# One new order for five engines, and no cleared spare words behind 71 indirect transfers, in an attention and expert kernel

## The chip, the cores and the metric

The kernel runs on one core of a Trainium2 chip. The metric is the device time of one launch in microseconds (us). Before the change it is 222.59 us, the median of three runs (222.12 to 223.31).

The engines are TensorE (PE, matrix products), VectorE (DVE), ScalarE (ACT), GpSimd (POOL) and SyncE (SP, which here only issues DMA). Each runs its own list of instructions in order, and semaphores tie the lists together.

## The reference

The input is normalised row by row. Causal attention over two batches of 2048 rows of 128, and a routed feed-forward layer of 8 experts, both read the normalised rows, and both are added to the input.

```python
def _L0_attn_ref(input_data, qk, ov):
    scores = jnp.einsum('bsd,de,bte->bst', input_data, qk, input_data) / SCALE
    scores = jnp.where(causal, scores, -jnp.inf)
    attn = jax.nn.softmax(scores, axis=-1)
    return jnp.einsum('bst,btd,de->bse', attn, input_data, ov)
...
def _L0_ffn_ref(input_features, centroids, ln_g, ln_b, w1, b1, w2, b2):
    x = input_features.reshape(-1, D)
    eid = jnp.argmax(x @ centroids.T, axis=-1)
    alpha = jax.nn.sigmoid(jnp.sum(x * centroids[eid], axis=-1, keepdims=True))
    xln = normalised(x) * ln_g[eid] + ln_b[eid]
    h = jax.nn.relu(xln @ w1[e] + b1[e])          # for the row's own expert e
    ffn = h @ w2[e] + b2[e]
    return x + alpha * ffn
...
x = L0_attn_input_data
xn = _layernorm(x, axis=-1)
x = x + _L0_attn_ref(xn, L0_attn_qk, L0_attn_ov) + _L0_ffn_ref(xn, ...)
```

The first listing lines are condensed: the layer applies only the expert that a row has chosen.

## The kernel before

The 4096 rows are 32 tiles of 128, in 8 groups of 4 tiles (4 groups for each batch).

**Attention.** A step n (0 to 79) takes one tile of keys against one group of 512 queries. In the order it is X.n (PE, scores in three 16-bit products), EH.n and EX.n (ACT, the exponential in 16 and in 32 bits), XL.n (DVE, the remainder `p_lo`, line 910), P.n and PB.n (PE, weights times values, lines 1343/1344 and 1351). A group of queries first needs its row maxima: M.b.g.i.c is one PE product, MR of the same indices its maximum by DVE (lines 892 and 896), RM.b.g gathers them, and SH/SHa write the shift into the queries. QT.b.g.f divides one half of a group by its sums and frees its banks. Keys, queries and values come by T, Q and V on PE, Ta, Qa, Va on ACT, Tl, Ql, Vl on DVE.

**Routing.** AFF and AFFr (PE), CH (DVE, choice of experts), CNT (PE), PL (DVE, each row's place in the sorted buffer). Then `send_rows` (SC.0 to SC.31 on POOL) scatters each tile of rows to `sorted_x` in HBM by an indirect DMA (line 684).

**Experts.** Once all 32 scatters have landed, SP issues transposing loads (`x2T`, line 526). For 39 tiles of sorted rows, HI.k is the first product (lines 1434 to 1436), RE.k and LO.k make its two 16-bit halves (ACT line 1166, DVE line 1018), OUT.k is the second product (lines 1456 to 1462), YS.j scales two tiles (ACT line 1174), and `store_rows` (SO.0 to SO.38 on POOL) scatters a tile to `sorted_y` (line 693). When all 39 have landed, SP loads the results back (line 568), Y.g adds a group (DVE line 937), and SP stores it.

**What sets the order.** ORDER is one list of 1120 entries, written out by hand or by a planner. Each engine walks the whole list and carries out the entries that are its own, so the list fixes the order within each engine and nothing between engines: semaphores do that. SP walks it too, for loads and clears that hang on W1, W2l and Z.

**The lines that the change touches.** `transfer_before` makes a scatter wait until the third scatter before it has landed (APART is 3). `pass_time` clears 600 words of `v_full`, in one partition, on POOL behind each of the 71 scatters; the next scatter stands behind that in POOL's list. `v_full` is no longer read by then: the first clear waits for that.

Other names of the prediction: VAR.g0.g1 are the statistics of groups g0 to g1 (DVE lines 778 and 781), LE their logarithm and root on ACT, RN the last step of the root (DVE for groups 0 to 1, POOL otherwise, lines 710 to 718), ROW the normalised rows by DVE (line 799), BIASa and BIAS the split of the biases (ACT lines 1095/1096, DVE lines 960/962), BASE a sum on POOL (line 641), MISC constants on POOL. W2l.e is the remainder of the second matrix of expert e on POOL (line 735): it reads two tensors in SBUF. W2.e is the ACT step ahead of it, and the matrices share three buffers, so SP loads the one of expert e+3 when W2l.e is done.

Of the kernel before, what the change touches and what calls it, by code (L numbers as in the profile page):

```python
# [1495 lines left out]
```

## Time and profile before

| | us |
|---|---|
| median of three runs | 222.59 |
| the profiled execution | 222.64 |
| its span, first to last instruction | 220.9 |
| PE busy | 205.3 (93%) |
| DVE busy | 176.3 (80%) |
| ACT busy | 155.2 (70%) |
| POOL busy | 155.0 (70%), of which the 71 clears 41.8 |

All later numbers are on the scale of the span, which starts at the first instruction. 1.7 us of the time lie around it. A busy PE includes the tail of each pipelined product, so a product of 512 columns is listed with 0.38 us although the next starts 0.22 us after it. To know the work of PE, take the distance from start to start.

### The profile page before, as it was taken

The page shows a single profiled execution, that of the slowest core. Times are in us where ns is not written, and L with a number is a line of the kernel's source. Part 1 is how long each engine was busy: PE and PEld are TensorE (multiplying, and loading weights), DVE is VectorE, ACT ScalarE, POOL GpSimd, SP SyncE. Part 2 cuts the span into 40 slices and gives each one's busy share as a digit, 9 for nine tenths or more (in the row PEclk, how much of TensorE's full clock was granted, in tenths as well). Part 3 has the DMA queues.
Part 4 walks back from the last instruction along what each step waited for, and adds up shares of the span by engine and source line. Part 5 has one row for each costly group of instructions (what it writes and reads, how often), then busy time and mean ns, then how long its engine had stood idle before and what let it go on. Part 6 is the DMA issues. An engine that isn't in the chain of part 4 may idle for free.

```text
span 220.9 us, 6878 instructions
## 1 busy us (share of the span) xinstructions
PE 205.3 (93%) x2428; PEld 159.0 (72%) x2428; DVE 176.3 (80%) x448; ACT 155.2 (70%) x346; POOL 155.0 (70%) x230
## 2 busy tenths in 40 slices
PE   7798875999979999999999989999999999999993
...
DVE  6799999898999999999999864576547674635995
...
GB/s 171 291 291 92 3 0 95 189 374 149 3 24 38 37 39 39 39 36 41 36 43 34 127 184 159 113 154 117 122 178 75 39 39 50 29 40 154 283 206 131
DMA packets 37601, 23.55 MB, mean 107 GB/s; under 512 B 12472, under 2 KB 34144, under 8 KB 37568
## 3 DMA queue, kind: packets, MB, share of 16 engines
...
q10 hardware_dynamic: 336, 0.14, 0.3%
...
## 4 chain that ended last, share of the span: by engine, by line
PE 77%; DVE 12%; ACT 4%; issue 4%; DMA 1%; SPq 1%; DVEq 0%; ACTq 0%
PE psum L1343 6%; PE psum L1300 6%; PE psum L1302 6%; PE psum L1301 6%; PE psum L1351 6%; PE psum L1344 6%; PE psum L1277 5%; PE psum L1462 4%; PE psum L1461 4%; PE psum L1460 4%; PE psum L1434 4%; PE psum L1436 4%; PE psum L1435 4%; PE psum L1260 3%; PE psum L1334 2%
## 5 line engine op out<-in xcount | busy, mean ns | idle before, releaser
L910 DVE TENSOR_TENSOR p_lo<-p_sb,p_hi 128x512 f16<-128x512 f32 (+1 forms) x68 | 42.0, 640 | 12.0 <-ACT p_sb L1050 11.8
L1044 ACT ACTIVATE p_hi<-psum 128x512 f16<-128x512 f32 (+1 forms) x68 | 37.1, 547 | 19.4 <-PE psum L1351 14.2
L1050 ACT ACTIVATE p_sb<-psum 128x512 f32<-128x512 f32 (+1 forms) x80 | 42.5, 538 | 6.8 <-PE psum L1334 6.7
L693 POOL DMA_INDIRECT sorted_y<-xn x39 | 38.6, 989 | 10.9 <-issue 5.4
L1018 DVE SCALAR_TENSOR_TENSOR h_lo<-psum,h_hi 128x512 f16<-128x512 f32 x39 | 26.8, 691 | 21.0 <-ACT h_hi L1166 19.4
L684 POOL DMA_INDIRECT sorted_x<-xr,pos x32 | 33.5, 1047 | 11.9 <-issue 11.4
L671 POOL MEMSET v_full<- 1x600 f32 x71 | 41.8, 589 | 0.0
L1166 ACT ACTIVATE h_hi<-psum 128x512 f16<-128x512 f32 x39 | 23.3, 597 | 19.6 <-PE psum L1436 17.3
L1343 PE MATMUL psum<-v_hi,p_hi 128*128 128x129 f16 x236 | 32.7, 220 | 1.2 <-DVE x_sb L927 1.2
L896 DVE TENSOR_REDUCE row_max<-psum 128x1 f32<-128x512 f32 x48 | 32.3, 684 | 1.6 <-PE psum L1277 1.1
L1344 PE MATMUL psum<-v_lo,p_hi 128*128 128x128 f16 x236 | 32.6, 219 | 0.0
L1277 PE MATMUL psum<-kT_hi,qT_hi 128*128 128x512 f16 (+3 forms) x80 | 26.3, 349 | 4.2 <-DVE row_max L896 1.8
L1434 PE MATMUL psum<-x2T,w_hl 128*128 128x128 f16 x156 | 28.0, 219 | 0.2 <-issue 0.2
L1462 PE MATMUL psum<-w_hl,h_lo 128*128 x156 | 28.1, 219 | 0.0
L1461 PE MATMUL psum<-w_hl,h_hi 128*128 x156 | 28.1, 219 | 0.0
L1460 PE MATMUL psum<-w_hl,h_hi 128*128 x156 | 28.1, 219 | 0.0
L1436 PE MATMUL psum<-x2T,w_hl 128*128 128x128 f16 x156 | 28.0, 219 | 0.0
L1435 PE MATMUL psum<-x2T,w_hl 128*128 128x128 f16 x156 | 28.0, 219 | 0.0
L1300 PE MATMUL psum<-qT_hi,kT_hi 128*128 128x512 f16 (+1 forms) x80 | 27.8, 347 | 0.0
L1302 PE MATMUL psum<-qT_hi,kT_lo 128*128 128x512 f16 (+1 forms) x80 | 27.8, 347 | 0.0
L1301 PE MATMUL psum<-qT_lo,kT_hi 128*128 128x512 f16 (+1 forms) x80 | 27.8, 347 | 0.0
L1343 PEld LDWEIGHTS psum<-v_hi,p_hi 128*128 128x128 f16 x236 | 23.0, 98 | 4.1 <-DVE x_sb L927 1.3
(189 smaller groups left out, 527.4 us busy)
## 6 DMA issues: line engine op xcount, KB each, us to landing
...
sorted_y<-xn POOLq DMA_INDIRECT x39
sorted_x<-xr,pos POOLq DMA_INDIRECT x32
```

What stands on the lines that cost most here:

```text
L671: pool.memset(idle, 0.0).then_inc(s_idle, 1)
L693: pool.indirect_dma_start(out=sorted_y[:, :], out_offset=bass.IndirectOffsetOnAxis(ap=tokens, axis=0), in_=xs[:, t % SLOTS, 0:P], in_offse ...
L910: v.tensor_tensor(p_lo[:, u, off:GW], p_sb[:, u, off:GW], p_hi[:, u, off:GW], ALU.subtract).then_inc(s_plo, 1)
L1044: a.activation(p_hi[:, u, off:GW], bank[SCORE[n % R]][:, off:GW], ACT.Exp, scale=SCALE).then_inc(s_exph, 1)
L1050: a.activation(p_sb[:, u, off:GW], bank[SCORE[n % R]][:, off:GW], ACT.Exp, scale=SCALE).then_inc(s_exp, 1)
L1277: mm(at[:, 0:w], qT_hi[:, q:q + P], kT_hi[:, k:k + w], start=True, stop=True).then_inc(s_mm, 1)
L1300: mm(at[:, off:GW], kT_hi[:, kk], qT_hi[:, q], start=True, stop=False)
L1301: mm(at[:, off:GW], kT_hi[:, kk], qT_lo[:, q], start=False, stop=False)
L1302: m = mm(at[:, off:GW], kT_lo[:, kk], qT_hi[:, q], start=False, stop=not diag)
L1343: mm(to[i], w, v_hi[:, kt, 0:P + 1], start=(j == 0 and i % 2 == 0), stop=False, skip_group_check=True)
L1344: mm(to[i][:, 0:P], w, v_lo[:, kt, :], start=False, stop=False, skip_group_check=True)
L1460: mm(to, h_hi[:, h, at], hi, start=False, stop=False, skip_group_check=True)
```

## The change

`pass_time`, its semaphore `s_idle`, the view `idle` and the constant IDLE go, and with them the 71 POOL memsets and the waits around them. ORDER has the same 1120 entries as before in another order, for all engines. No entry is added or dropped, and no function but the two scatter helpers changes.

```diff
 ORDER = entries("""
-VAR.0.1 VAR.1.2 BIASa LE.0.1 C0a AE.0 WU C0 C1 C2 T.0 W1.0 W1.1 BIAS RN.0.1 ROW.0.1 RN.1.2 MISC BASE.0 BASE.1 RN.2.3
-Vl.0 RN.3.4 BASE.2 RN.4.6 T.1 AE.1 AE.2 C1a LE.1.2 C2a Ta.0 W1h.0 W1h.1 Ta.1 W1l.0 Qa.0 Vf.0 LE.2.3 AE.3 W1l.1 AE.4
...
-M.0.3.0.3 P.6 AFFr.1.3 SH.0.2 M.0.3.3.2 X.11 V.2 P.7 CNT P.8 X.12 P.9 X.13 P.10 MR.0.3.3.2 Vl.2 QT.0.1.0 QT.0.1.1
-MR.0.3.1.3 XL.12 XL.13 MR.0.3.0.1 MR.0.3.2.2 Sl.1 MR.0.3.2.3 MR.0.3.3.3 MR.0.3.0.2 XL.14 MR.0.3.1.2 MR.0.3.3.0 X.14
-P.11 M.0.3.0.1 M.0.3.1.3 P.12 X.15 M.0.3.2.2 P.13 PB.12 M.0.3.3.3 M.0.3.2.3 X.16 M.0.3.0.2 PB.13 X.17 M.0.3.1.2 P.14
...
-SC.27 SC.28 SC.29 SC.30 SC.31 W2l.5 W2l.6 W2l.7 Sl.5 MR.1.1.3.0 XL.27 XL.28 XL.29 MR.1.1.1.1 MR.1.1.0.0 MR.1.1.3.1
...
-LO.1 M.1.3.3.0 X.51 PB.47 P.49 PB.48 P.50 PB.49 P.51 HI.0 PB.50 PB.51 HI.1 HI.2 OUT.0 LO.2 MR.1.3.1.0 MR.1.3.1.3 LO.3
...
-X.66 P.64 X.67 PB.63 XL.54 XL.55 XL.56 XL.57 XL.58 XL.59 XL.60 XL.61 XL.62 XL.63 XL.64 XL.65 XL.66 XL.67 Y.6 XL.68 Y.0
...
-SO.31 SO.32 SO.33 SO.34 SO.35 SO.36 SO.37 PB.70 X.73 P.72 PB.71 X.74 P.73 X.75 PB.72 X.76 PB.73 X.77 P.74 PB.74 X.78
-X.79 P.75 PB.75 P.76 PB.76 P.77 EH.77 EX.77 EH.78 EX.78 PB.77 P.78 P.79 PB.78 EH.79 EX.79 QT.1.3.0 QT.1.3.1 SO.38 PB.79
+VAR.0.1 VAR.1.2 LE.0.1 LE.1.2 C0a C1a BIASa C2a AE.0 Ta.0 Ta.1 AE.1 AE.2 AE.3 AE.4 W1h.0 LE.2.3 LE.3.4 W1h.1 AE.5 WU C0
+C1 C2 T.0 T.1 W1.0 W1.1 RN.0.1 ROW.0.1 C1v ROW.1.2 C2v BIAS Tl.0 VAR.2.3 VAR.3.4 Tl.1 MISC RN.1.2 RN.2.3 RN.3.4 BASE.0
...
+X.11 X.12 X.13 P.10 P.11 V.2 M.0.3.2.3 X.14 X.15 X.16 P.12 P.13 PB.12 PB.13 X.17 P.14 PB.14 P.15 M.0.3.0.0 M.0.3.0.1
...
+P.19 M.0.3.1.2 M.0.3.2.1 X.21 X.22 V.3 V.4 Q.4 PB.18 X.23 P.20 PB.19 PB.20 P.21 Vl.1 S.7 SC.0 SC.1 SC.2 W2l.2 W2l.3 SC.3
+SC.25 SC.26 SC.27 SC.28 SC.29 SC.30 SC.31 W2l.4 W2l.5 W2l.6 W2l.7 MR.1.0.1.0 Sl.4 RM.1.0 MR.1.1.0.1 MR.1.1.1.1 MR.1.1.3.1
...
+PB.44 PB.45 X.48 X.49 P.46 P.47 M.1.2.2.2 PB.46 X.50 X.51 P.48 PB.47 PB.48 REG M.1.2.1.2 P.49 P.50 P.51 HI.0 PB.49 PB.50
+PB.51 HI.1 HI.2 OUT.0 OUT.1 M.1.2.2.1 HI.3 HI.4 M.1.2.1.1 OUT.2 HI.5 OUT.3 HI.6 M.1.2.2.0 OUT.4 OUT.5 M.1.3.0.0 HI.7
...
+XL.59 XL.60 XL.61 XL.62 Y.6 Y.0 XL.63 XL.64 XL.65 XL.66 Y.7 Y.3 XL.67 XL.68 QT.1.2.0 XL.69 XL.70 QT.1.2.1 XL.71 XL.72
...
+PB.71 P.72 P.73 PB.72 X.75 X.76 PB.73 X.77 P.74 P.75 PB.74 X.78 PB.75 P.76 PB.76 X.79 P.77 PB.77 P.78 P.79 PB.78 EH.76
+EX.75 EX.76 EH.77 EH.78 EX.77 EX.78 EH.79 EX.79 QT.1.3.0 QT.1.3.1 SO.38 PB.79
 """)
...
-    IDLE = 600
...
-        idle = flat(v_full[:])[0:1, 0:IDLE]
...
-        s_idle = sem("s_idle")
...
-            pauses = [0]
-
-            def pass_time():
-
-                if pauses[0]:
-                    pool.wait_ge(s_idle, pauses[0])
-                else:
-                    pool.wait_ge(s_pv, N_FULL)
-                    pool.wait_ge(s_vhi, FULL)
-                    pool.wait_ge(s_vlop, FULL)
-                pool.memset(idle, 0.0).then_inc(s_idle, 1)
-                pauses[0] += 1
-
             def send_rows(i):
...
                 transfers.append((s_sent[i % SENT], 16 * (i // SENT + 1)))
-                pass_time()
 
             def store_rows(t):
...
                 transfers.append((s_yst[t % DUMPS], 16 * (t // DUMPS + 1)))
-                pass_time()
```

## Rows read from the trace of the kernel before

**Rows 1.** Page, part 2: busy tenths in 40 slices of 5.5 us.

```profile
PE   7798875999979999999999989999999999999993
DVE  6799999898999999999999864576547674635995
```

**Rows 2.** Windows by stage: length, then busy us (instructions) of each engine.

```profile
core 0: us, PE busy (x) PEld busy (x) DVE busy (x) ACT busy (x) POOL busy (x), PEclk, DMA share, GB/s
4.00:58.00 54.00, 46.38 (x342) 28.89 (x340) 49.99 (x176) 40.39 (x100) 35.05 (x70) 0.97 0.52 159
...
63.60:124.50 60.90, 60.38 (x659) 43.64 (x660) 58.34 (x134) 46.61 (x99) 52.79 (x65) 1.00 0.15 43
124.50:128.10 3.60, 2.31 (x39) 2.14 (x40) 3.16 (x9) 2.51 (x5) 1.16 (x1) 1.00 1.13 99
128.10:181.70 53.60, 53.59 (x930) 52.35 (x931) 32.45 (x55) 31.57 (x71) 45.87 (x59) 1.00 0.52 121
181.70:216.00 34.30, 34.30 (x405) 25.78 (x403) 22.76 (x42) 27.34 (x60) 15.55 (x20) 1.00 0.46 128
```

**Rows 3.** Timeline of PE, around P.12 and OUT.0: start us, duration us, line.

```profile
63.59 0.23 PE L1343 MATMUL psum<-v_hi,p_hi 128*128 128x129 f16 x1 [1.16 <-DVE x_sb L927]
...
64.06 0.38 PE L1300 MATMUL psum<-qT_hi,kT_hi 128*128 128x512 f16 x1
64.27 0.38 PE L1301 MATMUL psum<-qT_lo,kT_hi 128*128 128x512 f16 x1
...
128.10 0.10 PEld L1456 LDWEIGHTS psum<-b_hl,pick 128*128 x1 [1.46 <-issue]
```

**Rows 4.** Page, part 5: the cleared spare words.

```profile
L671 POOL MEMSET v_full<- 1x600 f32 x71 | 41.8, 589 | 0.0
```

**Rows 5.** Timeline of POOL: two scatters one after the other.

```profile
67.81 0.97 POOL L684 DMA_INDIRECT sorted_x<-xr,pos  x1 [0.17 <-issue]
...
69.53 0.97 POOL L684 DMA_INDIRECT sorted_x<-xr,pos  x1 [0.17 <-issue]
```

**Rows 6.** Line 684, POOL idle before it until an earlier scatter landed (us, times).

```profile
  DMA sorted_x<-xr,pos: 0.3, 2
```

**Rows 7.** Timeline of DVE, the first 20 us.

```profile
6.93 0.68 DVE L960 SCALAR_TENSOR_TENSOR b_hl<-b_sb,b_hi 16x512 f16<-16x512 f32 x1 [0.59 <-ACT b_hi L1096]
...
7.74 0.14 DVE L768 SCALAR_TENSOR_TENSOR nt<-mv,r 128x4 f32<-128x4 f32 x1
...
8.31 1.11 DVE L799 TENSOR_SCALAR xn<-x_sb,mv,r 128x127 f32<-128x127 f32 x4
...
11.21 3.01 DVE L799 TENSOR_SCALAR xn<-x_sb,mv,r 128x127 f32<-128x127 f32 x4
...
19.91 0.26 DVE L892 CUSTOM_DVE_ANT_0 masked<-psum,late_keys 128x128 f16<-128x128 f32 x1
```

**Rows 8.** Timeline of ACT, the wait for the biases.

```profile
5.88 0.72 ACT L1095 ACTIVATE b_hi<-b_sb,lower_half 16x512 f16<-16x512 f32 x1 [3.81 <-DMA b_sb<-in_L_ffn_b]
```

**Rows 9.** Timeline of POOL, its idle time before RN.1.2, and BASE.0.

```profile
9.34 0.24 POOL L710 TENSOR_SCALAR nt<-mv 128x4 f32<-128x4 f32 x1 [4.84 <-ACT r L1061]
...
12.41 1.16 POOL L641 TENSOR_TENSOR x_sb<-x_sb,xn 128x508 f32<-128x508 f32 x1
```

**Rows 10.** Timeline of DVE: start of PL, XL.47 to XL.49, LO.0 to LO.2.

```profile
58.02 0.16 DVE L849 TENSOR_SCALAR tiles_f<-psum 128x8 f32<-128x8 f32 x1
...
120.11 3.25 DVE L910 TENSOR_TENSOR p_lo<-p_sb,p_hi 128x512 f16<-128x512 f32 x3
...
126.24 1.93 DVE L1018 SCALAR_TENSOR_TENSOR h_lo<-psum,h_hi 128x512 f16<-128x512 f32 x3
```

**Rows 11.** Timeline of POOL: W2l.5 and W2l.6.

```profile
119.38 2.26 POOL L735 TENSOR_TENSOR w_hl<-w_raw,w_hl 128x512 f16<-128x512 f32 x2
```

**Rows 12.** Line 910 by itself, 62 to 80 us: duration ns minimum, median, maximum.

```profile
L910 DVE TENSOR_TENSOR p_lo<-p_sb,p_hi x8: 682/684/687, 63.8 to 78.5; 128x512 f16<-128x512 f32 x8
```

**Rows 13.** Timeline of SP: the eight loads of the results.

```profile
199.59 5.73 SPq L568 DMA_DIRECT2D xn<-sorted_y  x8
```

**Rows 14.** Timeline of ACT: EH.78, third exponential from the end.

```profile
215.73 0.38 ACT L1044 ACTIVATE p_hi<-psum 128x256 f16<-128x256 f32 x1 [0.41 <-PE psum L1351]
```

More of the change, by code:

```diff
@@ L129 @@
-X.79 P.75 PB.75 P.76 PB.76 P.77 EH.77 EX.77 EH.78 EX.78 PB.77 P.78 P.79 PB.78 EH.79 EX.79 QT.1.3.0 QT.1.3.1 SO.38 PB.79
+VAR.0.1 VAR.1.2 LE.0.1 LE.1.2 C0a C1a BIASa C2a AE.0 Ta.0 Ta.1 AE.1 AE.2 AE.3 AE.4 W1h.0 LE.2.3 LE.3.4 W1h.1 AE.5 WU C0
+C1 C2 T.0 T.1 W1.0 W1.1 RN.0.1 ROW.0.1 C1v ROW.1.2 C2v BIAS Tl.0 VAR.2.3 VAR.3.4 Tl.1 MISC RN.1.2 RN.2.3 RN.3.4 BASE.0
+BASE.1 BASE.2 RN.4.6 Vf.0 Qa.0 Qa.1 Z.0 RN.6.8 BASE.3 BASE.4 BASE.5 Vl.0 BASE.6 BASE.7 COL0 S.0 S.1 S.2 W2l.0 S.3 S.4
+S.5 S.6 W2l.1 VAR.4.6 Ql.0 Ql.1 MR.0.0.0.0 V.0 Q.0 Q.1 Z.1 Z.2 MR.0.0.2.0 MR.0.0.3.0 MR.0.0.1.0 VAR.6.8 RM.0.0 Z.3
@@ new lines @@
+M.0.0.0.0 W1b.0 W1b.1 M.0.0.2.0 M.0.0.3.0 M.0.0.1.0 W1.2 V.1 T.2 W1.3 M.0.1.0.1 W1b.2 M.0.1.1.1 M.0.1.2.0 Tl.2
+MR.0.1.0.1 MR.0.1.1.1 ROW.4.6 MR.0.1.3.1 MR.0.1.2.0 ROW.6.8 MR.0.1.1.0 MR.0.1.3.0 W1l.4 W1l.5 MR.0.1.2.1 Ql.2 MR.0.1.0.0
+R2 RM.0.1 MR.0.2.0.2 MR.0.2.2.1 MR.0.2.0.1 MR.0.2.3.1 MR.0.2.3.2 MR.0.2.2.0 W1l.0 W1l.1 XA.2 LE.4.6 W1h.2 Vf.1 Ta.2
+W1h.3 LE.6.8 W1l.2 W1l.3 Va.0 SHa.0.0 XA.3 W1h.4 W1h.5 Qa.2 EX.0 EX.1 EX.2 XA.5 SHa.0.1 XA.7 R2a EX.3 EX.4 W2.0 Ta.3
+Ta.4 EX.5 EX.6 Ta.5 Ta.6 Qa.3 Ta.7 W1b.3 M.0.1.3.1 SH.0.0 W1.4 W1.5 M.0.1.1.0 M.0.1.3.0 X.0 Q.2 M.0.1.2.1 X.1 X.2
@@ new lines @@
+M.0.3.1.2 M.0.3.2.1 X.21 X.22 V.3 V.4 Q.4 PB.18 X.23 P.20 PB.19 PB.20 P.21 Vl.1 S.7 SC.0 SC.1 SC.2 W2l.2 W2l.3 SC.3 SC.4
+SC.5 SC.6 SC.7 SC.8 SC.9 SC.10 SC.11 SC.12 SC.13 SC.14 SC.15 SC.16 SC.17 SC.18 SC.19 SC.20 SC.21 SC.22 SC.23 SC.24 SC.25
+SC.26 SC.27 SC.28 SC.29 SC.30 SC.31 W2l.4 W2l.5 W2l.6 W2l.7 MR.1.0.1.0 Sl.4 RM.1.0 MR.1.1.0.1 MR.1.1.1.1 MR.1.1.3.1
+XL.29 XL.30 XL.31 Sl.5 MR.1.1.1.0 Sl.6 XL.32 MR.1.1.2.1 MR.1.1.3.0 XL.33 MR.1.1.0.0 XL.34 XL.35 MR.1.1.2.0 RM.1.1 XL.36
+MR.1.2.0.0 MR.1.2.3.1 XL.37 XL.38 XL.39 MR.1.2.3.0 QT.0.3.0 QT.0.3.1 Sl.7 XL.40 XL.41 SH.0.3 P.22 P.23 V.5 V.6 V.7 PB.21
@@ new lines @@
+PB.44 PB.45 X.48 X.49 P.46 P.47 M.1.2.2.2 PB.46 X.50 X.51 P.48 PB.47 PB.48 REG M.1.2.1.2 P.49 P.50 P.51 HI.0 PB.49 PB.50
+PB.51 HI.1 HI.2 OUT.0 OUT.1 M.1.2.2.1 HI.3 HI.4 M.1.2.1.1 OUT.2 HI.5 OUT.3 HI.6 M.1.2.2.0 OUT.4 OUT.5 M.1.3.0.0 HI.7
+HI.8 OUT.6 HI.9 OUT.7 M.1.3.3.3 HI.10 OUT.8 HI.11 OUT.9 OUT.10 HI.12 HI.13 OUT.11 HI.14 OUT.12 HI.15 OUT.13 M.1.3.2.2
+HI.16 M.1.3.2.3 OUT.14 HI.17 OUT.15 HI.18 OUT.16 HI.19 OUT.17 HI.20 OUT.18 OUT.19 M.1.3.0.3 HI.21 M.1.3.1.3 OUT.20
+SH.1.2 HI.22 HI.23 OUT.21 HI.24 OUT.22 OUT.23 M.1.3.0.1 HI.25 HI.26 OUT.24 HI.27 OUT.25 EX.46 W1h.7 Qa.7 W2.5 EH.47
```

89 lines of the change are left out of this document (38 added, 51 removed).

## The prediction

> **What bounds the kernel now.** First the tenths of busy time [rows 1]: PE is near full from slice 13 (about 66 us) to slice 39, with one dent at slice 23. Ahead of that it isn't, but DVE is, from slice 3 on. Then the windows [rows 2]: from 4 to 58 us DVE is busy 49.99 of 54.00 and PE 46.38, and much of that is listed tails. From 63.6 to 124.5 both are full (60.38 and 58.34 of 60.90). From 128.1 to 216 PE has no gap and DVE has a third free. Then what ends PE's idle time [rows 3]: P.12 waits 1.16 us for DVE (QT.0.1.1 frees the banks of the sums), and OUT.0 starts at 128.10 after 1.46 us for the first LO and the loading of expert numbers.
>
> So I count PE's work. A product of 512 columns takes 0.216 us from start to start (64.06 to 64.27 [rows 3]), one of 128 columns a quarter of that. The same products are made before and after, so the end moves by two things alone: by how much work PE has done at a given time in the first 128 us, and by the tail. I use three marks: the start of PL on DVE (58.02 [rows 10]), P.12 (63.59) and OUT.0 (128.10 [rows 3]).
>
> **The change, part by part.**
>
> *The clears.* 71 memsets of 0.589 us, 41.8 us in all, leave POOL [rows 4]. A scatter follows the one before at 1.72 us: 0.97 for itself, 0.59 for the memset, 0.17 of waiting [rows 5]. Without the memset I take 0.97 + 0.17 = 1.14. The wait for the third scatter before bound twice in 32, for 0.3 us in all [rows 6], at a distance of three times 1.72. At 1.14 it may bind more, so the bounds of the spacing are 1.14 and 1.72. I take 1.2. That gives 38 us for 32 scatters instead of 55. From PL they would run to about 102, and HI.0 needs them at about 120: some 18 us of cover. Even at 1.72 they would end near 120. Worth by itself: 0. In the expert phase a tile takes PE 1.4 us (53.6 us [rows 2] for nearly 39 tiles), so the second set of scatters would follow PE and end near 187, and SP's loads would start near 189 instead of 199.59 [rows 13]. DVE wants them (Y.6 after XL.62) near 194, where before it stood after XL.67. Cover about 1 us, worth 0.
>
> Does DVE gain when the memsets go? XL takes 682/684/687 ns between memsets [rows 12]: no spread, no gain. The Trainium skill (SBUF — State Buffer, Who interferes with whom) says why: a DVE instruction with two SBUF inputs contends with a GpSimd instruction that reads SBUF, not with one that only writes. By that rule the clears are harmless, and W2l, which reads, isn't.
>
> *The head.* Now DVE waits 0.59 us for ACT's split of the biases [rows 7], which itself waits 3.81 us for its DMA [rows 8], and RN.0.1 starts behind BIAS at 7.74 [rows 7]. In the new order LE.0.1 and BIAS change places: RN.0.1 can start when VAR.1.2 is done, at about 6.3. That is 1.4 us sooner, of which 0.6 is a wait that vanishes and the rest is BIAS work moved behind. ROW.1.2 takes 3.01 us for four tiles where ROW.0.1 takes 1.11 [rows 7], and POOL's BASE.0 runs beside it [rows 9]. In the new order ROW.1.2 comes at about 9 us, when POOL waits between two RN (it sits idle for 4.84 us ahead of 9.34 now [rows 9], and MISC goes there). I take 1.11 for it: 1.9 less. Together 2.5. Walking DVE's list from there with a spacing of 0.6 us for each 512-column operation, I reach MR.0.0.0.0 at 18.1 with one more operation (Ql.1) done ahead of it, against 19.91 [rows 7]: 2.4 gained. Going on to PL, which has the same amount of DVE work ahead in both orders, I meet two new waits: CH.0 for the affinities (0.4) and the tighter ACT list around W2.3. I keep 1.6: PL at 56.4. Bounds: 0 (the chain over ACT takes it back) and 2.4.
>
> *More PE work ahead of P.12.* The new order puts X.15 and X.16 ahead of P.12: six products of 512 columns, 1.30 us, and 0.1 of maxima. This fills the 1.16 us wait [rows 3]. P.12 itself moves with QT.0.1.1 to about 62.0. So at P.12 PE's idle time so far would be 1.6 + 1.4 = 3.0 us less.
>
> *P.12 to OUT.0.* Seven M units and their MR go behind HI.0, with Ql.7 and RM.1.2 on DVE (1.4 us of PE, 3.2 of DVE ahead of LO.0). Against that, DVE starts this stretch with less done (X.15, X.16 and their XL are ahead on PE only). Adding up the entries, DVE needs 57.7 us from QT.0.1.1 to LO.0 where it needed 60.2, and PE 58.7 from P.12 to OUT.0 where it needed 61.5. Before, DVE lost 2.5 us in this stretch. I keep that loss: LO.0 at 62.0 + 57.7 + 2.5 = 122.2, and OUT.0 1.9 later as before (126.24 to 128.10 [rows 10, 3]): 124.1. PE's work ahead of OUT.0 is 1.4 less, so the net gain is 128.1 - 124.1 - 1.4 = 2.6 us.
>
> *W2l beside XL.* Before, three W2l stood behind the scatters. W2l.5 and W2l.6 ran from 119.38 to 121.64 [rows 11], and three XL took 3.25 us there [rows 10], where three spacings of 0.6 and a tail make 1.9: 1.4 lost. Now W2l.2 and W2l.3 stand after SC.2 and W2l.4 after SC.31, so three more run while XL runs. Bounds: 0 (DVE is at an operation that reads PSUM) and 3 x 1.4 = 4.2. I take 0.6, since DVE's loss counts only where PE waits for it and two of five of its operations there are XL.
>
> *After OUT.0.* PE has no gap in 88 us [rows 2], and the seven M units stand among 39 tiles, with DVE free for a third. Cost 0; if LO came late behind an MR it would be up to 0.6 at a time. *The tail.* X.79 stands behind P.75 to PB.76, 1.35 us of products later, and EH.78 ahead of EX.77. EH.78 already waits 0.41 for PE [rows 14]; then EX.77, EX.78, EH.79, EX.79, XL.79 and PB.79 must follow. I make it 0.3 longer; bounds 0 and 0.8.
>
> **Sum:** -2.6 + 0.6 + 0.3 = -1.7 us. The profiled execution took 222.64, so 220.9; the median of the runs (222.59) is the same to 0.1. Forecast 220.9.
>
> **The rivals.**
>
> *The head's gain is taken back (no change).* For it: ACT's list up to EX.8 is full too, and each step of my walk took the earliest time. Then PL starts at 58.0, P.12 near 63.5, and only the fuller PE list remains, 1.4 less 0.9 for tail and W2l: 222.1.
>
> *W2l against XL (slower).* Three XL beside two W2l lost 1.4 us [rows 10, 11]. (The Trainium skill, SBUF — State Buffer, Who interferes with whom, has this as a rule: whichever starts first holds the port, the other fully blocks. This trace agrees, with that one case.) If all three added W2l hit an XL while PE and DVE are both full, and those behind SC.31 hit as before, the cost is 4.2 instead of 0.6: 220.9 + 3.6 = 224.5. It decides from a loss of about 3.5 us on DVE between P.12 and LO.0 on top of the 2.5 it has. Against it: DVE's operations in between read PSUM, and only a start within the 1.13 us of a W2l counts. The list in pairs (two EH, then two EX) could lose time at the same place, by XL starting an ACT operation (0.5 us) later; the buffers are three, so I find no step where PE must wait for it, but it adds to this case.
>
> *The scatters don't come closer.* If the wait for the third before binds at each, the spacing stays near 1.7. The first set still has cover of about 0, the second ends near 192, Y.6 would wait 4 us, and PE with it for some 3 once its three buffers are full: 223.9.
>
> *The whole head gain holds and nothing is lost:* 2.4 instead of 1.6, and no W2l loss: 219.5.
>
> **How the numbers follow.** Forecast with its own spread (219.5 to 221.5, the last rival within): 0.55. Gain taken back (221.5 to 223): 0.22. W2l, or pairs, slower: 0.15, near 224.5. Scatters not closer: 0.08, near 223.9. The likeliest gives 220.9. The range reaches below to a head and a middle both better than walked (218.3) and above to the two slower cases in part (224.0), leaving out 0.2. A measurement of this kernel can tell about 0.5%, 1.1 us: faster means below 221.5, slower above 223.7. From the cases: faster 0.58, same 0.25, slower 0.17.
>
> **What would show each step.** ROW.1.2 at about 9 us in 1.1 us; PL near 56.4; P.12 near 62.0 without a wait; scatters 1.14 to 1.2 us apart, the first set ending near 102 and SP's loads of results near 189; OUT.0 near 124; no XL over 1.3 us. The prediction is wrong if PL starts at 58 or later, if PE waits between P.12 and HI.0 by more than 2 us, if an XL of 2 us appears more than once, or if Y.6 waits for its load.

## The result, and the profile after

The changed kernel takes 215.03 us (median of 4 runs, 214.78 to 216.25) where the kernel before took 222.57 beside it: ratio 0.967, 95% interval 0.963 to 0.971. The forecast of 220.9 had the direction right and was 5.9 us too slow, and 215.03 lies outside its range (218.3 to 224.0). The profiled execution is the slowest of the four, 216.25, with a span of 214.5. Executions more than 1.5% above the fastest of their kernel are left out of all medians and ratios below (one of b1, one of b3, four of c6).

Lines of the changed kernel stand 2 to 3 lower up to 655 and 16 to 18 lower behind (L910 is now L892, L799 is L781). First the page of the changed kernel, part 2, in 40 slices of 5.4 us (before: [rows 1]):

```profile
PE   7979999999999999999998799999999999999993
...
DVE  6899899999999999999998586646577574667784
...
PEclk9996999999999999999999999999999999999999
```

Slices are counted from 0. DVE is full from slice 2, and PE's dent comes in slices 21 and 22 instead of 23. PEclk (granted clock in tenths of 2.4 GHz) has a dip at slice 3. Then the windows by stage, as in [rows 2]:

```profile
core 0: us, PE busy (x) PEld busy (x) DVE busy (x) ACT busy (x) POOL busy (x), PEclk, DMA share, GB/s
4.00:52.60 48.60, 45.20 (x337) 29.12 (x335) 46.06 (x172) 36.78 (x92) 29.53 (x64) 0.96 0.46 141
52.60:57.90 5.30, 5.20 (x41) 3.18 (x39) 4.92 (x19) 5.02 (x13) 2.24 (x2) 1.00 0.54 175
57.90:116.10 58.20, 56.99 (x643) 42.18 (x644) 56.06 (x129) 48.30 (x103) 39.37 (x36) 1.00 0.20 60
116.10:120.00 3.90, 2.50 (x46) 2.33 (x44) 3.22 (x11) 3.01 (x6) 2.32 (x2) 1.00 0.94 190
120.00:173.30 53.30, 53.26 (x909) 51.32 (x910) 32.99 (x57) 29.73 (x69) 30.54 (x32) 1.00 0.50 115
```

The stretch up to PL is 5.4 us shorter, the one up to OUT.0 much as before. The marks are rows of the timelines of DVE (start of RN.0.1, ROW.0.1, ROW.1.2, ROW.6.8, PL) and PE (P.12, OUT.0), which answer to [rows 7], [rows 10] and [rows 3]; columns are start, duration, line and, in brackets, the idle time before:

```profile
6.00 0.16 DVE L750 SCALAR_TENSOR_TENSOR nt<-mv,r 128x4 f32<-128x4 f32 x1
6.59 1.11 DVE L781 TENSOR_SCALAR xn<-x_sb,mv,r 128x127 f32<-128x127 f32 x4
8.38 1.10 DVE L781 TENSOR_SCALAR xn<-x_sb,mv,r 128x127 f32<-128x127 f32 x4
25.78 1.11 DVE L781 TENSOR_SCALAR xn<-x_sb,mv,r 128x127 f32<-128x127 f32 x4
52.61 0.15 DVE L831 TENSOR_SCALAR tiles_f<-psum 128x8 f32<-128x8 f32 x1
```

```profile
57.92 0.23 PE L1325 MATMUL psum<-v_hi,p_hi 128*128 128x129 f16 x1
119.98 0.23 PE L1438 MATMUL psum<-b_hl,pick 128*128 128x128 f16 x1 [1.40 <-DVE h_lo L1000]
```

| mark, us from the start of the span | before | predicted | after |
|---|---|---|---|
| PL starts | 58.02 | 56.4 | 52.6 |
| P.12 | 63.59 | 62.0 | 57.92 |
| OUT.0 | 128.10 | 124.1 | 119.98 |
| OUT.0 to the end of the span | 92.8 | 94.5 | 94.5 |
| scatters, first set, last one starts | 117.8 | about 101 | 108.5 |
| SP's loads of results | 199.59 | 189 | 184.41 |

Behind P.12 the forecast of the marks holds almost to the tenth. Of the 5.9 us of the miss, 3.8 stand ahead of PL and 0.3 between PL and P.12; the other 1.8 are a term beside the marks (0.6) and the distance from the profiled execution to the median (1.2).

The scatters of the first set, by what GpSimd waited for before each, and the timeline of DVE and POOL where the pair W2l.4, W2l.5 meets XL (as in [rows 10, 11]):

```profile
L668 POOL DMA_INDIRECT sorted_x<-xr,pos x32: 954/958/1909, 62.5 to 108.5; - x32
...
  issue: 9.3, 13
  DMA sorted_x<-xr,pos: 5.9, 18
```

```profile
108.46 5.02 DVE L892 TENSOR_TENSOR p_lo<-p_sb,p_hi 128x512 f16<-128x512 f32 x4
```

```profile
109.44 2.28 POOL L717 TENSOR_TENSOR w_hl<-w_raw,w_hl 128x512 f16<-128x512 f32 x2
```

Four XL take 5.02 us where four alone take about 2.5. One of them, started at 109.11, takes 3166 ns by itself: the prediction wanted none over 1.3 us.

### The profile page after: what moved, and what is told of

The parts are those of the page before. It is cut to its first block, busy times and chain, and to the rows that moved or that the text cites. A ratio compares the mean times of both kernels' runs of the same rounds, so it can differ in the third digit from the quotient of the medians.

```text
span 214.5 us, 6806 instructions
## 1 busy us (share of the span) xinstructions
PE 203.2 (95%) x2428; PEld 158.5 (74%) x2428; DVE 173.0 (81%) x448; ACT 154.4 (72%) x346; POOL 113.7 (53%) x159
## 4 chain that ended last, share of the span: by engine, by line
PE 76%; DVE 17%; issue 5%; ACT 1%; DVEq 0%; ACTq 0%
PE psum L1333 6%; PE psum L1325 6%; PE psum L1259 6%; PE psum L1326 5%; PE psum L1284 5%; PE psum L1283 5%; PE psum L1282 5%; PE psum L1442 4%; PE psum L1444 4%; PE psum L1443 4%; PE psum L1418 4%; PE psum L1416 4%; PE psum L1417 4%; DVE row_max L878 3%; PE psum L1242 3%
## 5 line engine op out<-in xcount | busy, mean ns | idle before, releaser
L676 POOL DMA_INDIRECT sorted_y<-xn x39 | 37.4, 958 | 26.9 <-ACT xn L1156 14.7
L892 DVE TENSOR_TENSOR p_lo<-p_sb,p_hi 128x512 f16<-128x512 f32 (+1 forms) x68 | 41.9, 653 | 11.3 <-ACT p_sb L1032 11.0
L1026 ACT ACTIVATE p_hi<-psum 128x512 f16<-128x512 f32 (+1 forms) x68 | 35.7, 540 | 13.6 <-PE psum L1333 11.2
L668 POOL DMA_INDIRECT sorted_x<-xr,pos x32 | 34.8, 1088 | 15.5 <-issue 9.3
L1032 ACT ACTIVATE p_sb<-psum 128x512 f32<-128x512 f32 (+1 forms) x80 | 38.8, 537 | 3.0 <-PE psum L1286 3.0
L878 DVE TENSOR_REDUCE row_max<-psum 128x1 f32<-128x512 f32 x48 | 31.6, 681 | 1.0 <-PE psum L1259 0.7
L1325 PE MATMUL psum<-v_hi,p_hi 128*128 128x129 f16 x236 | 31.3, 220 | 0.1
L1326 PE MATMUL psum<-v_lo,p_hi 128*128 128x128 f16 x236 | 31.2, 219 | 0.0
L1259 PE MATMUL psum<-kT_hi,qT_hi 128*128 128x512 f16 (+3 forms) x80 | 25.0, 353 | 3.2 <-issue 1.0
L1416 PE MATMUL psum<-x2T,w_hl 128*128 128x128 f16 x156 | 27.6, 219 | 0.0
L1417 PE MATMUL psum<-x2T,w_hl 128*128 128x128 f16 x156 | 27.6, 219 | 0.0
L1418 PE MATMUL psum<-x2T,w_hl 128*128 128x128 f16 x156 | 27.6, 219 | 0.0
L1326 PEld LDWEIGHTS psum<-v_lo,p_hi 128*128 128x128 f16 x236 | 23.1, 98 | 1.6
```

What stands on the lines that cost most here:

```text
L676: pool.indirect_dma_start(out=sorted_y[:, :], out_offset=bass.IndirectOffsetOnAxis(ap=tokens, axis=0), in_=xs[:, t % SLOTS, 0:P], in_offse ...
L878: v.tensor_reduce(row_max[:, i, c:c + 1], bank[bank_of[unit]][:, 0:w], AX.X, ALU.max).then_inc(s_max, 1)
L892: v.tensor_tensor(p_lo[:, u, off:GW], p_sb[:, u, off:GW], p_hi[:, u, off:GW], ALU.subtract).then_inc(s_plo, 1)
L1032: a.activation(p_sb[:, u, off:GW], bank[SCORE[n % R]][:, off:GW], ACT.Exp, scale=SCALE).then_inc(s_exp, 1)
L1259: mm(at[:, 0:w], qT_hi[:, q:q + P], kT_hi[:, k:k + w], start=True, stop=True).then_inc(s_mm, 1)
L1325: mm(to[i], w, v_hi[:, kt, 0:P + 1], start=(j == 0 and i % 2 == 0), stop=False, skip_group_check=True)
```

## Experiments: the clears and the order, each without the other

**Only the clears go.**

```diff
 ORDER = entries("""
-(the new order)
+(the order of before, all 1120 entries)
 """)
```

> The changed kernel with the order of before: only the clears are gone. Theory (the clears are worth nothing by themselves; before, the last scatter of the first set starts at 117.8 and HI.0 at 124.5, with slack over the load): the scatters come 1.2 to 1.3 us apart and the first set ends near 106, but DVE's marks stay: Tl.0 and PL within 0.3 us of before (PL 58.0), HI.0 near 124.5, time 222.3 (221.5 to 223.0). Rival (the clears on GpSimd slow DVE or hold the start of the experts): 215 to 218.5, with OUT.0 4 us or more earlier than 128.1.

Measured 225.63 us, ratio 1.013 (1.011 to 1.015): 3 us slower than before. Neither theory had that. PL starts at 57.2, but there is a new loss at 110 to 118 us, in the timelines of POOL, DVE and PE of this run:

```profile
110.48 2.27 POOL L717 TENSOR_TENSOR w_hl<-w_raw,w_hl 128x512 f16<-128x512 f32 x2
```

```profile
110.08 3.44 DVE L892 TENSOR_TENSOR p_lo<-p_sb,p_hi 128x384 f16<-128x384 f32 x2
```

```profile
113.24 0.34 PE L1333 MATMUL psum<-v_hi,p_lo 128*128 128x129 f16 x3 [1.41 <-DVE p_lo L892]
...
114.17 1.32 PE L1242 MATMUL psum<-w_raw,A_e 128*128 128x512 f32 x2 [0.36 <-DVE w_hl L964]
115.29 0.63 PE L1244 MATMUL psum<-b_hl,pick_first 128*128 128x512 f16 x1
```

and its windows around that:

```profile
111.40:115.30 3.90, 2.12 (x18) 1.05 (x16) 3.87 (x7) 1.53 (x4) 1.35 (x2) 0.96 0.31 72
115.30:118.50 3.20, 3.20 (x13) 1.53 (x12) 1.80 (x7) 0.62 (x2) 0.00 (x0) 0.52 0.93 115
```

Without the clears the scatters end at 110.5, so W2l.5 and W2l.6 run from 110.48 instead of 119.38 [rows 11]. One XL is held through both (its own duration is 3103 ns), PE waits 1.41 us for it, is busy for only 2.12 of 3.90 us, and then gets 0.52 of its clock (that is, nearly all at 1.2 GHz) for 3.2 us: 512 columns take 0.63 us instead of 0.38.

**The clears are back, but where they delay only that pair.**

```diff
                 transfers.append((s_sent[i % SENT], 16 * (i // SENT + 1)))
-                pass_time()
+                if i == NT - 1:
+                    for _ in range(16):
+                        pass_time()
 ...
                 transfers.append((s_yst[t % DUMPS], 16 * (t // DUMPS + 1)))
-                pass_time()
```

> The old order with no clears between the scatters, but with 16 clears in a row (9.4 us) behind the last scatter of the first set, so that W2l.5 and W2l.6 come near 120 as they did before, and not near 110.5. With the old order and no clears at all they ran at 110.48, one XL took about 2.8 us, PE waited 1.41 for it and fell to 1.2 GHz for some 2.5 us: 225.6 against 222.6. Theory (that collision alone is the loss of 3 us): no XL over 1.9 us near 110, no fall of PE's clock there, time 221.5 to 222.6. Rival (scatters closer together are slower for the rest in another way): 224.5 or more.

Measured 222.86 us, ratio 1.000 (0.997 to 1.003), 0.26 above the top of the theory's interval and clearly not the rival. The windows of the same two stretches:

```profile
111.40:115.30 3.90, 3.90 (x39) 2.57 (x37) 3.86 (x10) 2.30 (x6) 3.64 (x6) 1.00 0.14 43
115.30:118.50 3.20, 3.20 (x29) 1.99 (x28) 2.93 (x10) 2.21 (x5) 2.91 (x6) 1.00 0.72 104
```

PE is busy throughout and keeps 2.4 GHz. So the 3 us are the collision and the clock after it, and the clears are worth nothing by themselves with the old order: taking them away only brings W2l to a worse place. The Trainium skill (SBUF — State Buffer, Who interferes with whom) says of GpSimd and a DVE operation with two SBUF inputs that the two can contend; the 3103 ns agree. Who started first did not decide it here: this XL started at 110.08, 0.40 us ahead of W2l.5 at 110.48, and it was XL that waited, while the two W2l took 1.17 and 1.15 us as ever. The same shows in all eight runs with an XL over 3 us (XL first by 0.33 to 0.41 us, though starts on POOL are rough), so the prediction's rule that the one that starts first blocks the other isn't borne out by them.

**Only the order changes.**

```diff
-                transfers.append(...)
+                transfers.append(...)
+                pass_time()
```

> The kernel of before with the new order: the clears stay. Theory (the order gives the gain up to PL, and the clears would then hold the start of the experts): PL stays near 52.6, but the scatters come 1.72 us apart from 62.5 and W2l.2 and W2l.3 stand among them, so the last starts near 118 instead of 108.5; the loads of the first expert tile follow and HI.0 starts near 123.5 instead of 116.1, so the time is 221 to 224, that is, the gain of the order shows only without the clears. Rival A (the order alone is the cause and the scatters have slack): 215 to 216.5, with HI.0 below 118. Rival B (DVE's marks up to 52.6 us need the clears gone): PL at 56 or later.

Measured 236.25 us, ratio 1.061 (1.058 to 1.065). PL starts at 51.1 and the last scatter at 119.9, as expected, but the loss of 21 us was nearly three times the expected one. The two halves of it were then taken apart.

```diff
 # in the first of the two runs send_rows alone has this line, in the second store_rows alone
+                pass_time()
```

> The new order with the clears kept in the first set of scatters only (32 of 71). With all 71 the kernel took 236.25 us: HI.0 waited 11.2 us for its load, started at 126.9 with TensorE at 1.2 GHz until about 131.8, and near the end PE waited 6.3 us behind Y.6. Theory (the two sets cost separately; the first set's clears cost the wait at HI.0 and the clock after it): last scatter near 120, HI.0 near 127, OUT.0 near 131.8, no wait at Y.6 beyond that, time 226 to 229. Rival (the first set has cover and the loss is the second set's): 215 to 217.5.

> The mirror: clears only in the second set (39 of 71). Theory: OUT.0 stays at 120, the second set takes 1.7 us for each scatter from 123.9, so its last starts near 190 instead of 182.0, the loads of results and Y.6 follow near 198 instead of 190.9, XL queues behind Y.6 and PE waits some 5 us with a drop of its clock: 221 to 224. Rival (the second set has cover): 215 to 217.

Clears in the first set alone: 228.13 us, ratio 1.024 (1.022 to 1.027), in the theory's interval. PE's wait ahead of HI.0 and the windows around it:

```profile
126.66 0.29 PE L1433 MATMUL psum<-x2T,w_hl 128*128 128x128 f16 x1 [11.04 <-DMA x2T<-sorted_x]
```

```profile
115.00:126.70 11.70, 0.66 (x13) 0.49 (x10) 0.89 (x5) 1.74 (x4) 9.24 (x11) 0.60 0.26 70
126.70:131.60 4.90, 4.57 (x42) 4.36 (x42) 2.95 (x9) 1.71 (x4) 1.15 (x1) 0.55 1.02 175
```

HI.0 comes 6.8 us behind the start of the last scatter (119.9). That isn't the scatter's own time alone: in the new order SP has a load of raw weights ahead of HI.0's load, and that load is issued just behind the end of W2l.4 (122.53), which stands right behind SC.31. Both in the timeline of SP of this run:

```profile
122.56 0.37 SPq L503 DMA_DIRECT2D w_raw<-in_L_ffn_w  x1
123.10 1.30 SPq L526 DMA_TRANSPOSE x2T<-sorted_x  x1
```

So HI.0's load is issued 3.2 us behind the start of the last scatter here, 2.7 in the changed kernel and 2.4 in the kernel before. It takes about 3 us to land: at 114.3 in the changed kernel, 1.8 ahead of HI.0 (116.1), and at 123.0 in the kernel before, 1.4 ahead of HI.0 (124.5). Before, too, there was this little cover: with a PE list that is ready for HI.0 some 8 us sooner, the clears use it up.

Clears in the second set alone: 224.98 us (ratio 1.008, 1.004 to 1.013; runs from 222.7 to 225.9), above the theory's interval of 221 to 224 in the median. Its profiled execution has a span of 222.9. The waits of DVE (Y.6, Y.7) and PE there:

```profile
195.61 0.69 DVE L936 TENSOR_TENSOR x_sb<-x_sb,xn 128x512 f32<-128x512 f32 x1 [6.06 <-DMA xn<-sorted_y]
198.51 0.69 DVE L936 TENSOR_TENSOR x_sb<-x_sb,xn 128x512 f32<-128x512 f32 x1 [2.21 <-DMA xn<-sorted_y]
```

```profile
199.46 0.29 PE L1350 MATMUL psum<-v_hi,p_lo 128*128 128x129 f16 x1 [7.83 <-DVE p_lo L909]
```

XL queues behind Y.6 on DVE, PE behind XL, and from 196 to 202 PE's granted clock is 0.54. The two halves together (13.1 and 10.0 over 215.03) make the 21.2 us of all 71 to within 2.

So the two parts of the change are worth -7.6 together, +3 (the clears alone) and +13.6 (the order alone).

## Experiments: what makes PL earlier

**Old head in the new order, and new head in the old order.**

```diff
 # a3: first entries of each engine as before
-VAR.0.1 VAR.1.2 LE.0.1 LE.1.2 C0a C1a BIASa C2a AE.0 Ta.0 Ta.1 AE.1 AE.2 ...
+VAR.0.1 VAR.1.2 BIASa LE.0.1 C0a AE.0 WU C0 C1 C2 T.0 W1.0 W1.1 BIAS RN.0.1 ROW.0.1 RN.1.2 MISC BASE.0 BASE.1 T.1 AE.1
+AE.2 C1a LE.1.2 C2a Ta.0 W1h.0 W1h.1 Ta.1 C2v C1v Tl.0 ROW.1.2 ...
 # a4: the reverse, all behind Tl.0, AE.2, RN.1.2 and W1.1 as before
```

> The changed kernel with the entries of the first 12 us (DVE to ROW.1.2, ACT to Ta.1, GpSimd to BASE.1, PE to T.1) back in the old order. After against before, DVE's time at an entry less the work listed ahead of it is 1.9 us better at Tl.0, 3.1 at R2 and 5.3 at PL. Theory (both halves count: the head gives about 2.5 us, the lists from 13 to 52 us give the rest by themselves): ROW.1.2 is at 11.2 and takes about 3 us again, PL near 55.0, time near 217.5 (216.5 to 218.5). Rival A (all is the head, and the later lists only pass it on): PL near 58, time 220.5 or more. Rival B (all is the later lists, and the head's gain would be caught up anyway): PL within 0.5 of 52.6, time below 216.

> The mirror: no clears, the order of before, but with the entries of the first 12 us (DVE to Tl.0, ACT to AE.2, GpSimd to RN.1.2, PE to W1.1) in the new order. Theory (both halves count): ROW.1.2 near 8.4 in 1.1 us, PL near 55.5 instead of 58.0, time near 220.0 (219.0 to 221.0). Rival A (all is the head): PL near 53, time 217 or less. Rival B (the head's gain is caught up again in the old lists): PL 57.5 or later, time 222 or more.

Old head: 218.23 us, ratio 0.984 (0.978 to 0.991), within the theory's interval, and the timeline of DVE shows ROW.1.2 held again and PL 1.9 us later than after:

```profile
11.38 3.01 DVE L781 TENSOR_SCALAR xn<-x_sb,mv,r 128x127 f32<-128x127 f32 x4
```

```profile
54.53 0.15 DVE L831 TENSOR_SCALAR tiles_f<-psum 128x8 f32<-128x8 f32 x1
```

The time is 3.2 us up, not 1.9. The profiled execution of the changed kernel had PE at 0.76 of its clock from 14 to 20 us and a3's at 0.97; where the new head and lists ran without it, PL is at 51.1 to 51.7, about 3 us ahead of this 54.5.

New head in the old lists: 224.14 us, where the old order without clears has 225.63. PL starts at 57.5, so nothing of the head is left there (57.2 without it). At ROW.4.6 the new head is still 1.45 us ahead of the old order without clears (28.21 against 29.66), although BASE.0 held BIAS for 1 us (1677 ns instead of 670): the gain goes between 30 and 57 us. DVE waits 1.2 us for PE's scores, 0.6 for kT_hi and 0.5 for the affinities on the way, together 1.1 more than in the old order without clears. Rival B was right for this run, the theory for the other: the head's gain lasts only with the new lists behind it.

**One cause put back: GpSimd's BASE beside ROW.1.2.**

```diff
-ROW.0.1 C1v ROW.1.2 C2v BIAS Tl.0 VAR.2.3 VAR.3.4 Tl.1 MISC RN.1.2 RN.2.3 RN.3.4 BASE.0 BASE.1
+ROW.0.1 C1v MISC RN.1.2 BASE.0 BASE.1 ROW.1.2 C2v BIAS Tl.0 VAR.2.3 VAR.3.4 Tl.1 RN.2.3 RN.3.4
```

> The changed kernel with one thing put back: GpSimd's BASE.0 and BASE.1 (1.16 us each, two SBUF inputs, back to back) stand beside DVE's ROW.1.2 again, here at about 8.4 us. Theory (the 3.01 us of ROW.1.2 before is one of its four operations held through both BASE, and that delay goes on to the end): ROW.1.2 takes 2 to 3 us again instead of 1.10, PL starts 1 to 1.9 us later than 52.6 and the kernel takes 216.0 to 217.0. Rival (ROW.1.2 was slow for another reason, or the delay is caught up at the next wait): ROW.1.2 1.1 us, or slow but PL within 0.3 of 52.6 and the time 215.0 (within 0.5).

Measured 217.53 us, ratio 0.977 (0.970 to 0.984), 0.5 above the theory's interval. The timelines of DVE and POOL, from the slowest execution (221.06):

```profile
8.31 1.94 DVE L781 TENSOR_SCALAR xn<-x_sb,mv,r 128x127 f32<-128x127 f32 x4
...
10.44 1.61 DVE L942 SCALAR_TENSOR_TENSOR b_hl<-b_sb,b_hi 16x512 f16<-16x512 f32 x1
```

```profile
8.23 1.18 POOL L638 TENSOR_TENSOR x_sb<-x_sb,xn 128x508 f32<-128x508 f32 x1
10.33 1.17 POOL L638 TENSOR_TENSOR x_sb<-x_sb,xn 128x508 f32<-128x508 f32 x1 [0.93 <-DVE xn L781]
```

BASE.1 waits for ROW.1.2 here, so the two BASE are apart and each holds one DVE operation: ROW.1.2 by 0.84, BIAS (1.61 instead of 0.67) by 0.94. PL starts at 54.7, 2.1 later. A hold of 1.8 us at 8 to 12 us is still whole at 52. The time is 2.5 us up, 0.4 more than PL's delay.

The expectation read the kernel before wrongly, though. The timeline of POOL there shows only BASE.0 beside ROW.1.2 (11.21 to 14.22 us), behind three steps of MISC, and BASE.1 once ROW.1.2 is over:

```profile
11.65 0.28 POOL L629 TENSOR_SCALAR_AFFINE_SELECT upper<-onesf 128x128 f16<-128x128 f32 x1
...
14.30 1.18 POOL L641 TENSOR_TENSOR x_sb<-x_sb,xn 128x508 f32<-128x508 f32 x1 [0.73 <-DVE xn L799]
```

In all five traces with the old head the held operation of ROW.1.2 ends 0.08 to 0.09 us behind BASE.0, whether it started at 11.21 (2445 ns) or at 12.17 (1511 ns). So the 1.9 us before are BASE.0 with what GpSimd did right ahead of it; b1 puts BASE.0 back and not MISC. Which steps of MISC hold and which don't is open.

**The two ROW free of holds in the old lists.**

```diff
-RN.6.8 W2l.0 W2l.1 BASE.4 BASE.5 BASE.6 BASE.7 W2l.2
+RN.6.8 BASE.6 BASE.7 BASE.4 BASE.5 W2l.0 W2l.1 W2l.2
```

> No clears, old order with the new head (this alone took 224.14), and also GpSimd's W2l.0 and W2l.1 moved from beside ROW.6.8 to behind BASE.4 to BASE.7 (which run as 6, 7, 4, 5). So neither ROW.1.2 nor ROW.6.8 is held. Theory (the holds are 2.9 us of what DVE saves up to PL, but the old lists give most of it back, since there DVE waits for PE's scores and PE for DVE's maxima from 31 to 58 us): ROW.6.8 in 1.1 us, PL 56.0 to 57.3, against 58.0 before and 52.6 with the new order. Rival (the holds are the gain, the lists only pass it on): PL at 55.0 or earlier.

Measured 227.79 us, PL at 62.0. Both ROW take 1.1 us, but the edit brought a wait of its own: ACT waits 5.10 us for the load of raw weights and DVE 4.3 us behind ACT. (As I read it, that load waits for the buffer that the later W2l.0 frees.) The run doesn't answer its question.

**The order cut at 28.5 us, in both directions.**

```diff
 # f1: entries started by 28.5 us in the new order, the rest as before; f2: the reverse
```

> No clears; the new order for what starts in the first 28.5 us (DVE to W1l.4, ACT to W1h.5, GpSimd to BASE.3, PE to M.0.1.2.1), the old order from there. Theory (the lists between 28 and 52 us are worth about 3 us of their own at PL, because the old ones make DVE and PE wait for each other): PL at 54.7 to 56.5 instead of 52.6 (51.3 to 52.6 in the runs of the new order so far), with waits of PE for DVE's maxima between 30 and 55 of 2 us and more. Rival (the gain is made before 28 us and kept): PL at 53.5 or earlier.

> The mirror: no clears; the old order for what starts in the first 28.5 us (DVE to Ql.2, ACT to Qa.2, GpSimd to BASE.3, PE to M.0.1.2.0), the new order from there. Theory (the late lists give about 3 us by themselves): PL at 54.5 to 55.5 against 58.0 before, and the kernel at 217.5 to 219. Rival (all is made before 28 us): PL at 57 or later.

| start of PL, us | R2 starts | PL starts | time |
|---|---|---|---|
| before | 30.6 | 58.0 | 222.6 |
| old order, no clears | 30.7 | 57.2 | 225.63 |
| new head, old lists | 29.2 | 57.5 | 224.14 |
| old to 28.5, then new | 33.9 | 56.4 | 219.96 |
| new to 28.5, then old | 28.8 | 55.6 | 223.56 |
| old head, new lists | 33.0 | 54.5 | 218.23 |
| new order (5 other runs: 51.1 to 51.7) | 31.1 | 52.6 | 215.03 |

(R2 is a short step of DVE, rows `ve<-r`. It has another place in the two lists, so compare it within one kind. The two runs cut at 28.5 us stood beside a kernel before of 223.69: their ratios are 0.983, 0.980 to 0.986, for old then new and 0.997, 0.994 to 1.001, for new then old.) Each half of the order alone brings PL 0.8 (old then new) and 1.6 us (new then old) below the old order without clears; both together bring 4.6, and 5.5 to 6.1 in the five other runs. f1 landed in the theory's interval, f2 missed it by 0.9 at PL and 1 us in time. What is shown: neither the head nor the lists make the gain by themselves.

**The later part.**

```diff
 # b3: new order to QT.0.1.1, P.12, EX.13 and S.7, from there as before
```

> No clears; the new order up to the sums' first release (DVE to QT.0.1.1, PE to P.12, ACT to EX.13, GpSimd to S.7), the old order from there. Theory (all of the order's gain lies ahead of P.12, and the rest of the new order gives nothing of its own, except that it chooses where W2l stands): P.12 at 57.9, and PE's time at OUT.0 less its listed work about 13 us as in the changed kernel, so 215 to 216; should W2l.5 and W2l.6 meet XL as they did with the old order and no clears, where PE then fell to 1.2 GHz for 3 us, then 218 to 220. Rival (the later part of the new order gives gain of its own): 217 or more with no XL over 1.3 us.

Measured 221.77 us, ratio 0.995 (0.991 to 0.999), where the theory had 215 to 216. PL is at 52.9, but right behind the cut PE waits 2.2 us for V's low half and 1.8 for a maximum, its clock falls for two slices, and X.24 starts at 81.2, as before. The cut made these waits, so this run gives no price for the later part. It does show that an earlier PL can be lost whole to the list behind it.

## Experiments: W2l and the scatters' spacing

```diff
 # b5: W2l one at a time
-SC.2 W2l.2 W2l.3 SC.3 ... SC.31 W2l.4 W2l.5 W2l.6 W2l.7
+W2l.2 W2l.3 Vl.1 S.7 SC.0 ... SC.6 W2l.4 ... SC.16 W2l.5 ... SC.24 W2l.6 ... SC.31 W2l.7
 # e2: the pair apart, two maxima behind LO.0
-Qa.7 W2.5 EH.47 ... EX.49
+Qa.7 EH.47 ... EX.49 W2.5
-MR.1.2.1.2 MR.1.2.2.2 QT.1.1.0 QT.1.1.1 LO.0
+QT.1.1.0 QT.1.1.1 LO.0 MR.1.2.1.2 MR.1.2.2.2
 # e4: W2.5 as in e2, and
-    APART = 3
+    APART = 4
```

> The changed kernel with GpSimd's W2l (1.14 us, two SBUF inputs) no longer back to back beside XL: W2l.2 and W2l.3 ahead of Vl.1, W2l.4, 5 and 6 one at a time behind SC.6, SC.16 and SC.24, with ACT's W2 moved to match. Theory (an XL that starts in a pair waits through both, 3.17 us for one at 108.46 in the changed kernel, while a single W2l costs at most 1.1): no XL over 1.9 us, DVE 1 to 2 us earlier at LO.0 (118.6), but PE has no wait there beyond OUT.0's 1.4, so at most 1.5 of it shows: 213.5 to 214.8. Rival (more W2l among XL hit more often, each near PE's limit): 215.5 to 217.

> A try to improve on the changed kernel: ACT's W2.5 behind EX.49, so that W2l.4 and W2l.5 no longer stand back to back at 109.4 (one XL took 3.17 us there), and the two maxima MR.1.2.1.2 and MR.1.2.2.2 behind LO.0 on DVE. Theory (DVE is the bound at LO.0, and OUT.0 waits 1.40 us for it): no XL over 1.9 us near 109, LO.0 near 117.9 instead of 118.6, OUT.0 near 119.3 instead of 120.0, time 213.8 to 214.8. Rival (single W2l are hit too, or PE's products wait for the two late maxima): 215 or more.

> The changed kernel with W2.5 behind EX.49 (as in the last try, whose time was that of the changed kernel), and a scatter waits for the fourth before it, not the third. Theory (the third-before wait is all of the 0.3 us that a scatter idles for, 18 times in 32, and there is cover for it): scatters 1.13 to 1.20 us apart where the changed kernel shows 1.26, last of the first set near 104.5 instead of 108.5, time within 0.5 of 215.0. Rival (four in flight land more slowly, and the loads behind them with them): HI.0 later than 116.1 and 216 or more.

W2l one at a time: 220.19 us, worse by 5 than the changed kernel and worse than its rival. Single W2l are hit as well (XL of 1927 ns at 73.9, 2057 at 90.2, 1276 at 114.8), and at each place the load of ACT's W2 is moved too. So the place counts, and not only the number in a row: in the changed kernel W2l.2 and W2l.3 stand at 66.3, where DVE works on maxima that it reads from PSUM, and no XL is over 0.7 us there. How the 5 us divide isn't settled.

The pair apart: 214.98, the same as the changed kernel (ratio to before 0.965, 0.963 to 0.967) and above the theory's 213.8 to 214.8. The longest XL fell to 2061 ns, and OUT.0 waits 1.33 us as before, now for the last W2l on POOL.

Four in flight: 215.30, the same again, with scatters no closer than before, against the theory's 1.13 to 1.20 us. The timeline of POOL in this run and in the changed kernel:

```profile
79.87 0.96 POOL L668 DMA_INDIRECT sorted_x<-xr,pos  x1 [0.30 <-issue]
81.13 0.98 POOL L668 DMA_INDIRECT sorted_x<-xr,pos  x1 [0.30 <-DMA sorted_x<-xr,pos]
```

```profile
81.93 0.96 POOL L668 DMA_INDIRECT sorted_x<-xr,pos  x1 [0.30 <-issue]
83.19 0.96 POOL L668 DMA_INDIRECT sorted_x<-xr,pos  x1 [0.30 <-DMA sorted_x<-xr,pos]
```

The 0.30 stays with a wait that allows one more, so it isn't that wait, whatever the profile puts it down to. 1.26 us is the least that a scatter takes here.

## Why the prediction was wrong, step by step

**The head, term "keep 1.6".** This is the failed step: PL came 5.4 us earlier. Two of its parts were right: BIAS behind RN.0.1 (6.00 against 6.3 predicted) and ROW.1.2 clear of MISC and BASE.0 (1.10 us at 8.38 against 1.11 at about 9). Of the 5.4 us, 1.9 are ROW.1.2; 0.9 are ROW.6.8, which took 2.03 us before with W2l.0 beside it (rows below) and which I had not looked at, though it is the same hold in the same trace; 1.2 are waits of DVE for ACT and PE that went from 2.6 to 1.4 us; 0.4 is the first load, which landed earlier by chance. About 1.0 is not itemized.

```profile
30.90 2.03 DVE L799 TENSOR_SCALAR xn<-x_sb,mv,r 128x127 f32<-128x127 f32 x4
```

```profile
31.68 2.33 POOL L735 TENSOR_TENSOR w_hl<-w_raw,w_hl 128x512 f16<-128x512 f32 x2 [2.06 <-ACT w_hl L1137]
```
My step took 2.5 at the head, walked on, and then took 0.8 back for new waits in the lists. These did not come: from 13 us to PL DVE waits once, 0.87 us at 22.39, and not at all for the affinities. a4 shows what the old lists do with such a gain (nothing left at PL) and a3 and b1 that the new ones keep it. That the walk took the time from there on for granted, with a deduction by feel, is the error: the lists between 20 and 52 us had to be walked to the end.

**P.12, and P.12 to OUT.0.** P.12 starts 5.3 us behind PL (predicted 5.6), after a wait under 0.3 us (predicted none). From there to OUT.0 62.1 us were predicted and 62.1 measured. That this fits to the tenth is in part luck: LO.0 came 60.6 us behind P.12 where the sum had 60.2, and OUT.0 1.4 behind LO.0 where it had 1.9. **W2l** was held at 0.6 beside that sum, and this counted it twice: the loss of 2.5 us that the sum kept for DVE holds such a pair already (1.4 us before). The pair at 109.44 cost DVE 2.5 us, but PE waited only 0.16 us for it, and with the pair apart (e2) the time is the same, so the term beside the sum was about 0.

**The tail**, 1.4 + 0.3, is right: 94.5 us from OUT.0 to the end.

**The clears, "worth 0".** Right for the kernel before (c1), and wrong as the sentence that even at 1.72 us the first set had cover. The last scatter would start near 119 and HI.0 needs 6 to 7 us from there, for which my sum had about 1. With PL at my 56.4 the order alone would already have lost; with PL at 52.6 it loses 21 us. The rival "not closer" named both mechanisms (HI.0's load, Y.6) but priced them at 3 us, without the fall of PE's clock.

**The spacing**, 1.26 us against 1.2, had the size right; the split into 0.97 + 0.17 + a wait didn't. The first set ends 7.5 us later than predicted, since two W2l and some scatters of 1.3 to 1.9 us lie in it: 31 spacings take 45.9 us, not 37.

**From 216.25 to 215.03.** The sum was made for one profiled execution, which happened to be before with its median. After, it is 1.2 above. The granted clock of PE from 14 to 20 us, in the changed kernel and in e4, which has the same head:

```profile
14.00:20.00 6.00, 4.36 (x12) 1.65 (x13) 5.95 (x32) 5.31 (x14) 5.17 (x14) 0.76 1.01 317
```

```profile
14.00:20.00 6.00, 4.35 (x27) 2.22 (x28) 5.97 (x33) 5.78 (x16) 5.17 (x14) 1.00 0.98 319
```

At 0.76 PL starts at 52.6, at 1.00 at 51.3. The spans of the changed kernel go much the same way: 214.5, 213.5, 213.1 and 213.0 us at a mean clock of 0.992, 0.997, 1.0 and 1.0, and a fifth execution 213.8 at 1.0. Clearer is f1, with ten: four at 1.0 take 222.1 to 222.2 us, six at 0.985 to 0.992 take 223.4 to 224.0. The miss is thus 4.1 (head and P.12), 0.6 (W2l) and 1.2 (the profiled run, which goes with its clock): 5.9.

The clock also tells the two heads apart, which I had overlooked. From 10 to 14 us it is 0.50 to 0.68 in all five traces with the old head and 1.00 in all others; before, and then after:

```profile
10.00:14.00 4.00, 3.67 (x5) 1.44 (x6) 3.87 (x8) 1.16 (x2) 3.40 (x12) 0.57 1.19 300
```

```profile
10.00:14.00 4.00, 3.61 (x21) 1.56 (x20) 3.93 (x20) 3.15 (x12) 0.76 (x4) 1.00 1.20 297
```

What of the gain comes from it no run shows.
